# A fused mixture-of-experts and feed-forward kernel: address table on VectorE, four small matmuls taken off TensorE, and the second weights' last half split by GpSimd

## The reference

```
# first layer: 4 experts and a shared one, D = 256, H = 1024; the top 2 of 4 experts per batch row
for e in range(4):
    h = gelu(x @ ew1[e] + eb1[e]);  out += w_be[:, e] * mask[e] * (h @ ew2[e] + eb2[e])
c = out + gelu(x @ sw1 + sb1) @ sw2 + sb2
...
# second layer: a shared gated unit (H = 128) on every token, 8 experts on M = 512 listed tokens
shared = ln(silu(c @ sw1.T + sb1) * (c @ sw2.T + sb2)) @ sw3.T + sb3
top1 = argmax(sigmoid(c[idx] @ eg_w.T + eg_b) + exp_bias)
shared[idx] = shared[idx] * w0 + expert_out[top1] * w1
return x + shared
```

## Time and profile before

| | |
|---|---|
| median of 3 runs | 551.83 us (551.66 to 552.08) |
| the profiled execution | 551.52 us, of which 549.6 us of span |
| TensorE busy | 540.3 us (98%), 5082 matmul instructions |
| VectorE, ScalarE, GpSimd busy | 397.2 us (72%), 264.4 us (48%), 168.5 us (31%) |
| the chain that ended last | TensorE 94% |

### The profile page before, as it was taken

How to read it: one execution, slowest core, us unless ns; L and a number is a source line. 1 busy time by engine, 2 the same in 40 slices (tenths; PEclk the granted TensorE clock), 3 DMA queues, 4 the chain that set the end, 5 groups by cost and what they waited for, 6 DMA issues and landing times.

```text
span 549.6 us, 16531 instructions
## 1 busy us (share of the span) xinstructions
PE 540.3 (98%) x5082; PEld 481.5 (88%) x5083; DVE 397.2 (72%) x1046; ACT 264.4 (48%) x664; POOL 168.5 (31%) x534
## 2 busy tenths in 40 slices
PE   9999999999999999999999999999999999999995
PEld 5888888886889999999999999999999999875874
DVE  4979988673965747767676585787885755577685
ACT  6665757652443544344343442443443433569670
POOL 0160000000464533534435334323234230095500
PEclk9999999999999999999999999999999999999998
DMA  8721245300100001323311000000000000094233
GB/s 266 251 117 57 97 151 151 100 2 1 40 1 3 2 3 49 124 100 116 117 41 41 1 2 2 2 3 2 2 4 2 3 4 4 4 343 149 87 124 114
DMA packets 28476, 36.88 MB, mean 67 GB/s; under 512 B 4762, under 2 KB 24115, under 8 KB 28132
## 3 DMA queue, kind: packets, MB, share of 16 engines
q1 hardware_dynamic: 28292, 35.57, 19.3%
q0 software_dynamic: 96, 0.20, 0.1%
HBM read 27.30 MB, written 8.53 MB: 65 GB/s over the span
## 4 chain that ended last, share of the span: by engine, by line
PE 94%; DVE 2%; issue 1%; DMA 1%; SPq 1%; POOL 0%; ACT 0%; ACTq 0%; DVEq 0%; POOLq 0%
PE ps_out L1251 42%; PE ps_hidden L1221 41%; PE ps_hidden L624 4%; PE ps_hidden L667 2%; DMA W<-in_xT 1%; PE ps_turn L650 1%; PE ps_small L650 1%; PE ps_out L637 1%; PE ps_out L1300 1%; DVE hbuf L1455 1%; DVE hbuf L1453 1%; PE ps_hidden L650 0%; SPq L1032 0%; DVE W L1438 0%; PE ps_out L689 0%
## 5 line engine op out<-in xcount | busy, mean ns | idle before, releaser
L1251 PE MATMUL ps_out<-hbuf,W 128*128 128x242 f16 (+4 forms) x2304 | 242.9, 266 | 0.5 <-DVE W L1438 0.5
L1251 PEld LDWEIGHTS ps_out<-hbuf,W 128*128 (+1 forms) x2304 | 218.4, 98 | 17.5 <-DVE W L1438 0.8
L1085 ACT ACTIVATE h<-ps_hidden,b 128x242 f32<-128x242 f32 (+3 forms) x384 | 151.6, 461 | 67.2 <-PE ps_hidden L1221 64.3
L1893 POOL COPY xs<-X 128x88 f16 x334 | 111.4, 382 | 174.3 <-PE ps_hidden L1221 169.1
L1221 PE MATMUL ps_hidden<-xs,W 128*128 128x242 f16 (+2 forms) x1536 | 156.1, 262 | 1.1 <-issue 1.1
L1221 PEld LDWEIGHTS ps_hidden<-xs,W 128*128 (+1 forms) x1536 | 143.3, 98 | 9.2 <-issue 1.6
L1455 DVE TENSOR_TENSOR hbuf<-h,hbuf 128x484 f16<-128x484 f32 (+4 forms) x192 | 127.6, 664 | 7.5
L1746 DVE SCALAR_TENSOR_TENSOR acc<-ytmp,wrow,acc 128x44 f32 (+1 forms) x334 | 62.9, 261 | 80.7 <-ACT ytmp L1175 69.6
L1453 DVE CAST hbuf<-h 128x484 f16<-128x484 f32 (+4 forms) x192 | 83.9, 437 | 13.4 <-ACT h L1085 12.2
L1221 PE MATMUL ps_hidden<-X,W 128*128 128x256 f16 (+1 forms) x768 | 87.5, 274 | 0.0
L1175 ACT ACTIVATE ytmp<-ps_out,b 128x242 f32<-128x242 f32 (+3 forms) x64 | 25.4, 448 | 124.6 <-PE ps_out L1251 124.6
(11 more groups left out here) (317 smaller groups left out, 297.3 us busy)
## 6 DMA issues: line engine op xcount, KB each, us to landing
stage<-in_ew SPq DMA_DIRECT2D x16, 512.0 KB, 3.8
stage<-in_xR SPq DMA_DIRECT2D x8, 512.0 KB, 3.8
moved_rows<-stage SPq DMA_DIRECT2D x8, 512.0 KB, 2.6
X<-moved_rows SPq DMA_DIRECT2D x8, 512.0 KB, 9.7
out_rows<-X SPq DMA_DIRECT2D x16, 256.0 KB, 2.2
W<-in_xT SPq DMA_DIRECT2D x7, 512.0 KB, 9.0
W<-in_fw SPq DMA_DIRECT2D x1, 2304.0 KB, 11.3
W<-in_sw SPq DMA_DIRECT2D x4, 256.0 KB, 3.5
```

The lines of the kernel that those rows point to most:

```text
L1085: i = nc.scalar.activation(h32[:, j, k * size:(k + 1) * size], ps1[j][:, k * size:(k + 1) * size], ACT.Gelu_apprx_tanh, bias=b1[:, bass.ds ...
L1251: mm = pe.matmul(out, w2(e, wp, hb, db), h, start=(n == 0), stop=(n == 3 * HB - 1))
L1893: i = nc.gpsimd.tensor_copy(xs[:, parity, :, j * SEG:(j + 1) * SEG], X[:, :, bass.ds(cols[j], SEG)])
```

## The change

It does five things.

1. GpSimd makes both halves of the last piece of the second weights: it multiplies by WS in place, casts to the high half, and subtracts. `open_high(6, 8)` and `open_low(6, 8)` become `(6, 7)`. `output(0)` waits for `w2_lo`.
2. `hidden(0)` waits for high halves at the start of a column block, and for the low ones only ahead of the matmuls that read them.
3. The parts of the table that don't need the selection matmuls are computed by VectorE ahead of them. The addresses in x are computed by VectorE ahead of `splits(12)`, and GpSimd only reads them.
4. The two biases `b3e` and `b3s` are added by VectorE (the latter loaded as 128 equal rows) and not by a matmul each.
5. The keys are written to DRAM and read back into every partition; `key()` and its four matmuls go, and VectorE compares from SBUF instead of PSUM.

```diff
@@ SyncE, in stage2_loads, after all rows are out
+            sp.wait_ge(key_ready, 1)
+            sp.dma_start(a["keys"].rearrange("(g p) -> p g", p=P), f4[:, 8, :],
+                         allow_slow_non_contiguous=True).then_inc(key_out, 16)
+            sp.wait_ge(key_out, 16)
+            sp.dma_start(keyrow, a["keys"].partition_broadcast(P)).then_inc(key_in, 16)
@@ SyncE, loads
-            for dst, src in ((w30, a["w3t"][:, 0:D]), (b3s, a["b3s"]), (b3e, a["b3e"]),
+            for dst, src in ((w30, a["w3t"][:, 0:D]), (b3s, a["b3s"].partition_broadcast(P)), (b3e, a["b3e"]),
@@ ScalarE
-            open_high(6, 8)
+            open_high(6, 7)
...
-                    nc.scalar.activation(ce8w, psy[1][0:FE, 0:D], ACT.Copy).then_inc(ce_made, 1)
-            act.wait_ge(c0_mm, 1)
-            nc.scalar.activation(c0b, psg[:, D:2 * D], ACT.Copy).then_inc(c0_ready, 1)
@@ TensorE, hidden
-                        pe.wait_ge(w_split, j + 2)
+                        pe.wait_ge(start_hi, j + 2)
...
                         for wp, xp in ((0, 0), (0, 1), (1, 0)):
+                            if first and k == 0 and (wp == 1 or xp == 1):
+                                pe.wait_ge(w_split, j + 2 if wp == 1 else 1)
@@ TensorE, ahead of output(0)
-            pe.wait_ge(w_split, 8)
+            pe.wait_ge(w_split, 7)
+            pe.wait_ge(w2_lo, 1)
@@ TensorE, small matmuls
-                    pe.matmul(psy[1][0:FE, 0:D], ident[0:FE, 0:FE], b3e, start=False, stop=True).then_inc(ce_mm, 1)
...
-            pe.matmul(psg[:, D:2 * D], betrep, w30, start=True, stop=False)
-            pe.matmul(psg[:, D:2 * D], onesm[0:1, :], b3s, start=False, stop=True).then_inc(c0_mm, 1)
+            pe.matmul(psg[:, D:2 * D], betrep, w30, start=True, stop=True).then_inc(c0_mm, 1)
...
-            def key():
-                pe.wait_ge(key_ready, 1)
-                for g in range(MG):
-                    mm = pe.matmul(pst[:, g * P:(g + 1) * P], onesm[:, :], kdiag[:, g, :], start=True, stop=True)
-                mm.then_inc(key_mm, 1)
@@ VectorE, ahead of splits(12)
+            link(nc.vector.tensor_scalar(srow, fa, 1.0 / BS, 0.5 / BS - 0.5, ALU.mult, ALU.add))
+            link(nc.vector.tensor_scalar(srow, srow, ROUND, None, ALU.add))
+            link(nc.vector.tensor_scalar(srow, srow, -ROUND, None, ALU.add))
+            link(nc.vector.scalar_tensor_tensor(fa, srow, -2.0, fa, ALU.mult, ALU.add))
+            nc.vector.tensor_scalar(xtab[:, :], fa, float(TOK), None, ALU.min).then_inc(slots_ready, 1)
+            splits(12, 0)
             splits(13, 1)
+            dve.wait_ge(c0_mm, 1)
+            nc.vector.tensor_tensor(c0b, psg[:, D:2 * D], b3s, ALU.add).then_inc(c0_ready, 1)
@@ GpSimd, first of all
+            w2src, w2hi, w2lo = opening[7][2:5]
+            pool.wait_ge(start_in[7], 16)
+            link(nc.gpsimd.tensor_scalar(w2src, w2src, WS, None, ALU.mult))
+            link(nc.gpsimd.tensor_copy(w2hi, w2src))
+            nc.gpsimd.tensor_tensor(w2lo, w2src, w2hi, ALU.subtract).then_inc(w2_lo, 1)
...
-            link(nc.gpsimd.tensor_scalar(whole, row, 1.0 / BS, 0.5 / BS - 0.5, ALU.mult, ALU.add))
-            link(nc.gpsimd.tensor_scalar(whole, whole, ROUND, None, ALU.add))
```

More of the change, by code:

```diff
@@ L165, in program @@
         late = [acc[:, 1, q * CB * BS:(q + 1) * CB * BS] for q in range(12, 15)]
-        b3e, betrep, mean0, b3s = late[0][0:FE, 0:D], late[1][:, 0:P], late[1][:, P:2 * P], late[2][0:1, 0:D]
+        b3e, betrep, mean0, b3s = late[0][0:FE, 0:D], late[1][:, 0:P], late[1][:, P:2 * P], late[2][:, 0:D]
         ident2 = acc[0:NB, 1, 15 * CB * BS:15 * CB * BS + P]
@@ L208, in program @@
         start_hi = sem("start_hi")
+        w2_lo = sem("w2_lo")
         w_split = sem("w_split")
@@ L1139, in _ @@
             weigh(0, ((4, 5), (6,)))
-            act.wait_ge(w_split, 8)
+            act.wait_ge(w_split, 7)
+            act.wait_ge(w2_lo, 1)
             weigh(1, ((7,), ()))
@@ L1299, in _ @@
                     for f in range(FE):
-                        pe.matmul(psy[1][0:FE, 0:D], betm[:, f, :], w3e[:, f, :], start=(f == 0), stop=False)
-                    pe.matmul(psy[1][0:FE, 0:D], ident[0:FE, 0:FE], b3e, start=False, stop=True).then_inc(ce_mm, 1)
+                        mm = pe.matmul(psy[1][0:FE, 0:D], betm[:, f, :], w3e[:, f, :],
+                                       start=(f == 0), stop=(f == FE - 1))
+                    mm.then_inc(ce_mm, 1)
                 pe.wait_ge(hot_ready, u + 1)
@@ L1365, in step @@
                     output(r + (R0 - 1), before, (r - 1) % 2, RC, between)
-                if r == 14:
-                    key()
                 if r == 18:
@@ L1489, in _ @@
                 if g == 0:
-                    open_low(6, 8)
+                    open_low(6, 7)
                 else:
@@ L1606, in _ @@
                                         ALU.subtract).then_inc(hot_ready, 1)
+            tv = tab[:, 0:NR * ROW].rearrange("p (r k) -> p r k", k=ROW)
+            above, evens = yw[0:1, 414:414 + NR], yw[0:1, 450:450 + (NR + 1) // 2]
+            link(nc.vector.tensor_scalar(above, siota[0:1, 0:NR], G[0:1, 19, 1:2], None, ALU.is_ge))
+            for e in range(2, E):
+                link(nc.vector.scalar_tensor_tensor(above, siota[0:1, 0:NR], G[0:1, 19, e:e + 1], above,
+                                                    ALU.is_ge, ALU.add))
+            link(nc.vector.tensor_copy(tv[:, :, SLOTS], above))
+            total, even = G[0:1, 27, 0:1], G[0:1, 27, 1:2]
+            link(nc.vector.tensor_tensor(total, G[0:1, 19, E - 1:E], G[0:1, 18, E - 1:E], ALU.add))
+            link(nc.vector.tensor_scalar(evens, siota[0:1, 0:NR:2], total, None, ALU.is_lt))
+            link(nc.vector.tensor_reduce(even, evens, AX.X, ALU.add))
+            link(nc.vector.tensor_scalar(even, even, -2.0, 1.0, ALU.mult, ALU.add))
+            link(nc.vector.tensor_tensor(even, even, total, ALU.add))
+            link(nc.vector.tensor_scalar(total, total, -2.0, None, ALU.add))
+            link(nc.vector.tensor_scalar(G[0:1, 27, 2:3], even, -1.0, 1.0, ALU.mult, ALU.add))
+            link(nc.vector.tensor_copy(tab[:, NR * ROW:NR * ROW + 2], G[0:1, 27, 0:2]))
+            link(nc.vector.tensor_copy(tab[:, NR * ROW + 3:NR * ROW + 4], G[0:1, 27, 2:3]))
             dve.wait_ge(v_hi, 1)
-            dve.wait_ge(ce_made, 1)
+            nc.vector.tensor_tensor(ce8w, psy[1][0:FE, 0:D], b3e, ALU.add).then_inc(ce_made, 1)
             nc.vector.tensor_tensor(V0[:, 1, :], psy[1][:, D:2 * D], V0[:, 0, :], ALU.subtract).then_inc(v_taken, 1)
@@ L1624, in _ @@
-            for e in range(1, E):
-                link(nc.vector.tensor_scalar(ce[:, e, :], siota[0:1, 0:NR], G[0:1, 19, e:e + 1], None, ALU.is_ge))
-            link(nc.vector.tensor_tensor(ce[:, 1, :], ce[:, 1, :], ce[:, 2, :], ALU.add))
-            link(nc.vector.tensor_tensor(ce[:, 1, :], ce[:, 1, :], ce[:, 3, :], ALU.add))
-            link(nc.vector.tensor_copy(tv[:, :, SLOTS], ce[:, 1, :]))
-            total, even = G[0:1, 27, 0:1], G[0:1, 27, 1:2]
-            link(nc.vector.tensor_tensor(total, G[0:1, 19, E - 1:E], G[0:1, 18, E - 1:E], ALU.add))
@@ L1904, in _ @@
             stage_lead(1)
-            pool.wait_ge(c0_mm, 1)
+            pool.wait_ge(c0_ready, 1)
             link(nc.gpsimd.memset(slate, 0.0))
@@ L1958 @@
     a["ce8"] = nc.dram_tensor("expert_rows", (FE, D), F32, kind="Internal").ap()
+    a["keys"] = nc.dram_tensor("row_keys", (M,), F32, kind="Internal").ap()
     a["gcols"] = nc.dram_tensor("gather_columns", (MX,), I32, kind="Internal").ap()
```

40 lines of the change are left out of this document (9 added, 31 removed).

## The result

The changed kernel took 554.52 us (median of 9 runs, 552.43 to 556.25); the kernel before took 551.66 (9 runs, 551.34 to 553.81). The ratio is 1.0044, with a 95% interval of 1.0023 to 1.0065: slower by 0.44%, 2.4 us (the medians alone differ by 2.9). The forecast was 551.7, with a range of 549.8 to 553.9. The profiled execution took 554.52 us, of which 552.6 of span, 3.0 more than before. In the groups of runs further down, one execution of *columns between* and one of the kernel before took over 940 us at a mean granted clock of 0.557; the medians given there count them, the ratios don't.

A forecast was written before the change was run, and what follows sets the result against it. The prediction took TensorE to bound the kernel, doing nearly all the chain. From 551.52 us it added 3.0 of opening stall, subtracted 3.0 of savings and added 0.2 to 0.3 for the median: 551.7 us, range 549.8 to 553.9.

The forecast's parts named there:

- with the clock kept: Main forecast: opening stall of 2.4 to 3.7 us paid by 3.0 of savings, clock not falling; chance 0.45.
- the savings: Work and waits taken off TensorE: `key()` 0.90, expert bias matmul 0.52, shared bias matmul and wait 1.57; 2.99 us.
- the 551.5 of the sum: Whole kernel: profiled 551.52 us plus 3.0 of stall minus 3.0 of savings, before 0.2 to 0.3 for the median.
- VectorE loses one 1.17 us low half and ends the other before 19, so GpSimd is last: Opening: `output(0)` would wait for GpSimd's subtraction, ending at 20.8, not for VectorE.
- a few tenths each: Opening: loss of VectorE and GpSimd working side by side, up to 1 us.
- The size of the stall: Opening: GpSimd's split takes 8.1 us from 12.7, so `output(0)` starts at 20.9 instead of 17.89, +3.0 us.
- The clock falls in the new stall: Rival, opening: matmuls behind the stall run at 1.2 GHz, costing 0 to 2.4, taken as 1.7; 553.4 us; chance 0.28.
- From a stall of about 3 us: Threshold at which the clock rival decides; the earlier trace's clock fell 3.0 us after the last matmul.
- The 1.57: Before the first expert chunk: shared bias matmul and the wait behind it go, 1.57 us saved.
- The table was in time: Before `splits(12)`: five added VectorE instructions, 0.57 each; `output(12)` late by 0 to 1.0, taken as 0; lateness rival 0.05.
- The 0.3 of the first products: Opening: starting on high halves gains 0.3 us, all lost in the wait of `output(0)`.
- The rival of a quick GpSimd: Rival, opening: GpSimd's multiply at the quicker rate, stall +0.6 or less; 549.4 down to 548.5 us; chance 0.15.

The follow-up runs named there:

- columns between: Kernel without the split, its nine one-column products near the end laid between the twelve matmuls ahead of them: 552.04 us, ratio 0.9991 to before.
- the split alone: The kernel before with only GpSimd making both halves of the last second weights put in: 558.26 us, ratio 1.0093 to before.
- filler: The changed kernel with 16 unread 512-column matmuls ahead of the wait of `output(0)`: 553.0 us, ratio 0.9996 to before.
- two operations: The changed kernel with GpSimd's multiply given a second operation that does nothing (plus 0): 553.21 us, ratio 0.9999 to before.
- low half earlier: The changed kernel with VectorE's remaining low half moved ahead of the last block of the first chunk's split: 552.63 us, ratio 1.0013 to before.
- the filler at the end: Kernel without the split, with four unread 256-column products between the nine one-column products near the end: 548.68 us, ratio 0.9927 to before.
- the kernel without the split: The changed kernel with both halves of the last second weights on ScalarE and VectorE again: 549.5 us, 0.9935; run again 548.18 us, 0.9928.
- the kernel with the bias undone: Kernel without the split, with both bias matmuls on TensorE and ScalarE's copies back, address table still on VectorE: 550.69 us, ratio 0.9963 to before.
- the mark: The kernel without the split, run a second time beside kernels that undo single savings: 548.18 us, ratio 0.9928 to before.

## Why the prediction was wrong

**Two steps failed.** The one that made the time wrong is "with the clock kept": the forecast put the low clock behind the new stall at nothing, and didn't know of one at the end. Each cost 1.67 us in the profiled execution, 3.3 together. The later start of `output(0)` was 0.3 less than forecast and the savings 0.2 more, which leaves 2.9 of the 3.0 by which that execution missed the 551.5 of the sum. The clock has its own paragraphs below.

The other step gave the wrong mechanism and left the time alone: "VectorE loses one 1.17 us low half and ends the other before 19, so GpSimd is last". VectorE was last, at 20.57. It lost 2.25 us beside the multiply and the cast, which put its low half beside the subtraction, and 1.9 more there (3.14 for 1.22). The prediction had seen one VectorE instruction take 0.8 more beside GpSimd's subtraction and took that for "a few tenths each". It is not an amount but an end: VectorE's instruction ends after the subtraction's, however long that is, as the five profiles with a subtraction in the opening (the changed kernel, the split alone, filler, two operations, low half earlier) show, and as the one where GpSimd only multiplies and casts shows from the other side. The Trainium skill has this: SBUF — State Buffer, section "Who interferes with whom", says that a VectorE instruction with two inputs in SBUF contends with a GpSimd instruction that reads SBUF, and that the port pair they share is an exclusive lock. Where VectorE subtracts, the rows beside GpSimd's subtraction agree with it; the instruction held in *two operations* is a cast, with one input, and that sentence doesn't cover it. The multiply's rows agree only in part: beside its 3.15 us a VectorE subtraction still took 0.69 at 14.36.

**The size of the stall** came out right by luck. GpSimd took 6.8 us in all where 8.1 were forecast: multiply 3.15 (forecast 3.8), cast 1.11 (1.5), subtraction 2.44 (2.6). The landing was as forecast, 12.6 against 12.7. That alone would have let `output(0)` start at 19.5 or 19.6; VectorE's delay gave back 1.1, and the start was 20.62 against 20.9. Against 17.60, where the second x would have put it in that execution (9.54 + 8.06), the stall costs 3.0.

**The clock** decided. It was the rival with 0.28, "The clock falls in the new stall", and its price of 1.7 was right: `output(0)` took 1.67 longer. Its 553.4 was still 1.1 short. The lower speed was read from the opening's matmuls of 512 columns, 0.44 us each; the granted clock of the profile stands at 1.00 there (1.25 to 6.00 us), so it is only their length that bears it, against 0.23 each for the filler's. The profiles with an idle of 2.77, 2.91, 3.31, 3.46 and 3.49 us ahead of `output(0)` all show the lower clock behind it; those with 0.18 to 1.12, and the filler, don't; no profile has an idle in between there. It isn't certain in every execution: of the 51 of these five kernels, five had a mean clock of 0.998 or 0.999 and so no low stretch while TensorE had work. "From a stall of about 3 us" was a fair reading of the earlier trace rows, and the forecast stall of 3.8 was beyond it: the reading should have given this rival most of the chance.

**The clock at the end** wasn't in the prediction at all. By the mean clock it falls in some executions of every kernel without the filler at the end, of the kernel before too. In the traces it costs 1.67; the two kinds of executions of the kernel without the split lie 1.6 us apart in one group (548.7 and 550.4 on average) and 2.1 in the other (548.0 and 550.1). The profiled execution of before had none of it and that of after did, so of the 3.0 us between the two profiles 1.7 are of this kind. How much of the 2.4 us of the ratio is, the record doesn't say: before's nine runs have no clocks on record, and all but two of them lie below 552.1. Three of the nine executions of the changed kernel (555.46 to 556.25 us) had a mean clock of 0.989, lower than the 0.992 of the profiled one with its two low stretches while TensorE had work. So the clock was low for longer there, and no profile shows where.

**The savings** held: 0.61, 1.67 and 0.89 against 0.52, 1.57 and 0.90. The 1.57 was one number for two causes, the matmul (0.7) and the idle that the address table's place caused (0.87), and the kernel with the bias undone took them apart. The table was in time: VectorE's five added instructions took 0.36 to 0.57 and not 0.57 each, and `output(12)` did not wait. GpSimd's copies, which the prediction had done by 153, came later: they began at 153.30 and thirteen took 6.64, 0.51 each where the earlier trace rows has 0.29, and were still done before the chunk at 161.91. Nothing waited for the keys. The 0.3 of the first products was swallowed, as the prediction said, and the mark's profile shows by what: VectorE's chain from the second x, which is taken up 8 us earlier.

**The rival of a quick GpSimd** was wrong for this form and right for the other. The Trainium skill's sentence in GPSIMD Engine Reference, section 4.1, that one-input work is "roughly line-rate", fits the cast and the multiply with two operations, 1.10 each; the multiply with one operation took 2.82 to 3.15 in five profiles. And even with the quick form the kernel only matched before: the price of the split is in what it holds up.

## What to carry to other kernels

When work goes to GpSimd beside a busy VectorE, cost it as if VectorE stood still for the length of GpSimd's subtraction (2.2 to 2.5 us here), add what its one-input instructions take from VectorE (1.6 to 2.3 us here), and ask which of VectorE's instructions that will be and who waits for it. A new stall of TensorE (2.8 to 3.5 us in five profiles here) costs its length and then, in most executions, the slower matmuls behind it; matmuls that nobody reads, put into the wait, took that second part away. Leave the split out and keep the rest: that version is 0.65 to 0.72% faster than before in two separate groups, and 1.1% faster than the change as a whole, by the ratios.

## What the hardware showed that I had not expected

- A multiply by a constant on GpSimd, 128x1024 fp32, takes 2.82 to 3.15 us with one operation and 1.10 with a second one that does nothing.
- VectorE's instructions beside GpSimd's 2.17 to 2.45 us subtraction: 3.14 for 1.2, 2.49 for 0.69, 2.35 for 0.42. Beside its cast of 1.1: 1.40 for 0.69.
- The lower clock can come when the stall is over: in the changed kernel it ends at 20.62, the mean granted clock is 0.95 over 20 to 22 us and 0.50 over the next two. In the kernel with two operations it is 0.50 from 20 us on, where the stall ends at 20.13.
- TensorE can be shown as busy without a gap and still fall to 1.2 GHz, as behind the 18 records of one-column products at 537.23, which count as 2.17 us of work. What brings it about there is open.
